# The lead of the row scores over the key scores in quad 0: fourteen units at first, two more per block

## The reference

```python
q, k, v = split_heads(x @ Wq.T + bq), ...          # 16 heads of 16 columns
q, k = rope(q), rope(k)
att = where(tril, einsum('bhqd,bhkd->bhqk', q, k) / 4, -inf)
y = einsum('bhqk,bhkd->bhqd', softmax(att), v)     # then @ Wo.T + bo
x = layernorm(x + y)
h = silu(x @ w1.T * s1) * (x @ w2.T * s2)          # 256 -> 1024
h = gelu(h @ h1.T * s)                             # 1024 -> 1024
h = gelu(h @ h2.T * s)                             # 1024 -> 1024
x = layernorm(x + h @ w3.T * s3)                   # 1024 -> 256
```

## Time and profile before

| | |
|---|---|
| median of three runs | 2791.91 us |
| the profiled execution's own time | 2795.36 us |
| its span | 2793.6 us |
| PE busy | 2729.1 us (98%) |
| VectorE (DVE) busy | 1899.9 us (68%) |
| ScalarE (ACT) busy | 1348.4 us (48%) |
| mean granted clock of PE | 0.989 |

### The profile page before, as it was taken

One profiled execution on the slowest core, in us unless ns is written; L12 is line 12 of the kernel. 1 busy time (PEld: TensorE's weight loads), 2 busy tenths in 40 slices (PEclk: granted clock), 3 DMA queues, 4 the chain that ended last, 5 costly groups with the idle time before them and its releaser, 6 DMA issues.

```text
span 2793.6 us, 39368 instructions
## 1 busy us (share of the span) xinstructions
PE 2729.1 (98%) x14880; PEld 1424.9 (51%) x14880; DVE 1899.9 (68%) x4003; ACT 1348.4 (48%) x2641; POOL 138.3 (5%) x206
## 2 busy tenths in 40 slices
PE   8899999999999999999999999999999999999998
PEld 4423333333333333333323333588888887888887
DVE  6999999888888888888887774633333352443343
ACT  4436666777776777777777776411111111000100
POOL 3300110001100001100000000000000000000000
PEclk9979999999999999999999999999999999999999
DMA  7731110001110011110001000411111132121100
GB/s 217 204 74 39 30 30 26 3 15 32 29 43 6 5 33 32 30 34 3 1 3 39 19 5 9 118 58 58 58 58 58 43 128 108 46 82 54 45 16 23
DMA packets 95613, 133.47 MB, mean 48 GB/s; under 512 B 31462, under 2 KB 69094, under 8 KB 91718
## 3 DMA queue, kind: packets, MB, share of 16 engines
q1 hardware_dynamic: 81452, 96.25, 10.7%
q0 software_dynamic: 6336, 23.34, 3.8%
q10 hardware_dynamic: 7648, 11.54, 1.5%
HBM read 83.77 MB, written 47.32 MB: 47 GB/s over the span
## 4 chain that ended last, share of the span: by engine, by line
PE 88%; DVE 6%; issue 2%; ACT 1%; DMA 1%; SPq 0%; ACTq 0%; POOLq 0%; POOL 0%; DVEq 0%
PE wi_f L984 19%; PE at_o L533 18%; PE at_row L498 17%; PE at_key L512 16%; PE na_h L1202 13%; PE na_y L1214 3%; DVE at_segmax L584 3%; DVE fr_masked L580 1%; DMA values<-pr_vals 1%; ACT at_probs L648 1%; PE at_key L515 1%; PE wi_p L833 1%; DVE pr_parts L252 0%; DVE pr_full L248 0%; PE pr_main L130 0%
## 5 line engine op out<-in xcount | busy, mean ns | idle before, releaser
L648 ACT ACTIVATE at_probs<-at_key 128x512 f32<-128x512 f32 (+3 forms) x2304 | 1127.3, 567 | 502.4 <-PE at_key L512 353.2
L584 DVE TENSOR_REDUCE at_segmax<-at_row 128x1 f32<-128x512 f32 x1792 | 1142.8, 684 | 169.2 <-PE at_row L498 164.9
L512 PE MATMUL at_key<-fr_q_stack,fr_k_stack 99*128 99x512 bf16 (+3 forms) x1152 | 415.0, 365 | 1.3 <-ACT at_probs L648 1.0
L498 PE MATMUL at_row<-fr_k_stack,fr_q_stack 96*128 96x512 bf16 (+3 forms) x1152 | 404.6, 376 | 10.8 <-DVE at_mask L612 5.5
L498 PE MATMUL at_row<-at_k_stack,at_q_stack 96*128 96x512 bf16 (+3 forms) x1152 | 408.1, 364 | 1.8 <-DVE at_segmax L584 1.1
L512 PE MATMUL at_key<-at_q_stack,at_k_stack 99*128 99x512 bf16 (+3 forms) x1152 | 402.2, 364 | 7.5 <-ACT at_probs L648 6.9
L1202 PE MATMUL na_h<-fr_h,fr_h2w_h 128*128 128x512 f32 x1024 | 322.1, 396 | 1.4 <-DVE fr_h L730 1.4
L533 PE MATMUL at_o<-at_probs,fr_values 128*32 128x512 f32 (+3 forms) x2304 | 289.0, 574 | 0.0
L533 PE MATMUL at_o<-at_probs,at_values 128*32 128x512 f32 (+3 forms) x2304 | 287.9, 572 | 0.0
L580 DVE CUSTOM_DVE_ANT_0 fr_masked<-at_row,fr_causal 128x384 f32<-128x384 f32 (+3 forms) x512 | 243.8, 483 | 45.1 <-PE at_row L498 44.7
L498 PEld LDWEIGHTS at_row<-fr_k_stack,fr_q_stack 96*128 96x128 bf16 x1152 | 110.3, 99 | 308.3 <-DVE at_segmax L584 160.1
(11 more groups left out here) (121 smaller groups left out, 2558.1 us busy)
## 6 DMA issues: line engine op xcount, KB each, us to landing
hidden<-wi_h SPq DMA_DIRECT2D x64, 256.0 KB, 2.0
na_h2f<-hidden SPq DMA_DIRECT2D x8, 1024.0 KB, 7.7
q_parts<-pr_parts SPq DMA_DIRECT2D x48, 128.0 KB, 2.4
k_parts<-pr_parts SPq DMA_DIRECT2D x48, 128.0 KB, 3.3
at_q_stack<-q_parts POOLq DMA_DIRECT2D x48, 128.0 KB, 3.5
at_k_stack<-k_parts POOLq DMA_DIRECT2D x48, 128.0 KB, 3.8
values<-pr_vals SPq DMA_DIRECT2D x32, 136.0 KB, 3.3
outputs<-at_outs SPq DMA_DIRECT2D x128, 34.0 KB
```

The source lines that it names most:

```text
L498: last = nc.tensor.matmul(bank[:, 0:w], qst[u][0:SROWS, c, h, i * P:(i + 1) * P], kst[u][0:SROWS, h, s * CH:s * CH + w], start=True, stop= ...
L512: last = nc.tensor.matmul(bank[:, q0:CH], kst[u][0:SROWS + PARTS, h, j * P:(j + 1) * P], qst[u][0:SROWS + PARTS, c, h, q0:CH], start=True, ...
L584: nc.vector.tensor_reduce(segmax[:, n % 2, h * TPC + i, s:s + 1], row_ps[r % RING_R][:, 0:w], op=ALU.max, axis=AX.X).then_inc(rows_taken, 1)
L648: nc.scalar.activation(probs[:, g % RING_P, h, q0:CH], key_ps[m % RING_K][:, q0:CH], ACT.Exp).then_inc(probs_ready, 1)
```

## The change

One constant is added, and the slack in the goal of `rows_before_keys` is the smaller of the old one and fourteen units plus two units for every block (n is the number of the key block). From block 7 on it is the old 28 units.

```diff
 SLACK = 28 * CH
+FIRST_SLACK = 14 * CH
 FIRST_EARLY = 3
...
-            goal = min(total, key_cols + lead + SLACK)
+            goal = min(total, key_cols + lead + min(SLACK, FIRST_SLACK + n * CH * 2))
```

## The result

The changed kernel takes 2804.63 us, the median of six runs (2803.88 to 2806.04); the kernel before took 2792.13 beside it (2791.44 to 2796.06). The ratio is 1.0044, 95% interval 1.0033 to 1.0055: 12.5 us slower. The forecast was 2799.0 with a range to 2803.5, so the direction was right and the size was not.

The account below looks back on a forecast made before the run. The prediction took VectorE to bound the beginning of the attention stage, with PE taking over gradually. Hole 7.3 less 1.0 saved gave +6.3, plus 0.7 for the clock: +7.0 us, forecast 2799.0, range 2790.5 to 2803.5.

Parts of the forecast that it names:

- Step 1: Before the first key score: fourteen rows fewer in front save nothing; it starts 0 to 0.5 us earlier, taken as 0.
- Step 2: Before the first key score: DVE idles from 151.15 to about 158.4 after row unit 36, 7.3 us.
- Step 3: Blocks 0 to 6: 6,912 missing columns repaid, 8.3 us at DVE's price, 3.0 at PE's; net with the hole +6.3 us.
- the saving of 1.0 us: DVE idle that extra rows take away: 0.64 us in blocks 5 and 6, another 0.4 us in block 1.
- Rival A: Quad 0: PE bounds the repayment, missing rows cost 3.0 us plus a 0.5 us restart; +3.5, 2795.4 us; chance 0.15.
- Step 4: Maxima of blocks 1 to 6: fewer units before their keys still cover store and reload; cost 0.
- Step 5: Near 166, block 0's keys: closing operations of block 1 delay the rise of PE's clock; +0.7 us, ends 0 and +3.4.
- Rival C: Quad 0: clock low through most of block 0, or one more fall near a closing operation; +10.4, 2802.3 us; chance 0.16.
- Rival B: Quad 0: not slower, as the clock's falls at 186 and 230 vanish; -0.2, 2791.7 us; chance 0.12.

Follow-up runs that it names:

- the late shift: Changed kernel with 32 matmuls of 128 columns, results unused, on PE in front of the first key unit of quad 1: 2804.32 us, ratio 1.0036.
- the store first: Changed kernel with SyncE's loads of chunk 3 moved from in front of the first maxima to behind their reload: 2797.64 us, ratio 1.0020.
- The pair with filler: Sixteen unused matmuls ahead of each transpose of maxima, in the changed kernel (2817.74 us, ratio 1.0095) and in the kernel before (2815.78 us, 1.0084).
- the filler in the hole: Changed kernel with 56 matmuls of 128 columns, results unused, on PE in front of the first key unit: 2804.20 us, ratio 1.0046.
- the split load of the values: Changed kernel with chunk 3's loads behind the first maxima and quad 0's values loaded in two parts, the second behind the maxima: 2795.37 us, ratio 1.0009.

## Why the prediction was right in kind and short in size

**What bounds quad 0: shown.** VectorE's work, plus its idle time. Filling its idle with moved row units made quad 0 shorter, and holes made it longer.

**Step 1, start of the keys: right.** The first key score gained nothing: 24.06 us after the first row matmul, against 23.67 and 24.41 in the two executions of before. The cause is also shown: it waits for maxima that stand behind the loads of chunk 3. Without those loads in front it came at 18.65. The fixed cost of 2.0 us that the prediction quotes from the Trainium skill, "DMA: Bandwidth & Descriptors", section on the anatomy of one DMA, stands there for DMAs that GpSimd issues, and this reload is SyncE's. In the changed kernel the first key score starts 1.8 us after the reload is issued, so the 1.3 us of the trace was the better term.

**Step 2, the hole: right.** 7.3 us forecast, 7.79 measured. What a hole costs is also shown: 3.5, 4.3 and 8.3 us for holes of 3.3, 4.2 and 7.5.

**Step 3, the repayment: at VectorE's price, and the saving of 1.0 us did not come.** At the start of block 1 the changed plan is 6,272 columns short. In the execution with the late shift blocks 1 to 6 took 7.4 us longer than in the second execution of before, and so they did with the store first: 1.2 ns per column, VectorE's price. (Both have a fall between 194 and 202 that the kernel before lacks, with 1.4 to 1.5 us of idle of VectorE, and lack its fall at 230, worth 1.4; the two nearly cancel.) Quad 0 as a whole grew by 472.78 - 462.16 = 10.6 us, and DVE's waits by 36.1 - 26.3 = 9.8 us. The bookkeeping by idle time holds to 0.8 us here and to 1.4 us between the two executions of before (28.6 and 26.3 us of waits for 3.7 us of time). The pair with filler gives 5.9 at a hole of 6.13, a saving of 0.2 us where I had 1.0. Rival A (the repayment at PE's price, +3.5) is out.

**Step 4, later maxima: right.** PE waited for maxima once, at block 0.

**Step 5, PE's clock: this step failed.** I valued it at +0.7, with 3.4 as the upper end, and I counted one place. The runs show falls at three places of quad 0 and one of quad 1. In quad 0 those at 170 and 286 cost some 2.4 us together; the one at 198 is not priced by itself, and VectorE's idle in its stretch, 1.54 us, is about its upper end. The kernel before also loses 1.4 at 230, which the changed one does not: some 2.5 net. In quad 1, which I left out because the order of the work does not change there, the difference between the kernels grows by 3.0 us at the output store behind the fall (2.8 from mark 2 to mark 3). Together that is over 5 us where the sum had 0.7. Rival C, one more fall near a closing operation, had +10.4 for quad 0 and came nearest there (10.6); it too had nothing for quad 1. Rival B's sign is there as well: the clock stays at 0.98 or more from 186 to 198 and at 1.00 at 230, so both falls of the first profile are gone. But the one behind the closing operations of block 2 is back at 198, where these operations now stand, and those at 170 and 286 are new; B's gain did not come. The Trainium skill, "TensorE: Matmul & The Clock Gate", part 1, says that activity releases the clock and that the throttled state is the default. The rows from 162 to 170 show the clock rise once keys and values run; the fall at 170 came although PE had been busy 2.10 of the 4 us before it. I had used the section only for the stretch in front of the key.

**The base.** The profile that I read had a fall worth 3.7 us in quad 0 that the second profile does not have. Counted against that one execution, quad 0 grew by 6.9 us, which looks like the forecast of +7.0, but only because a fall in either kernel stands in the count; counted against the second one it grew by 10.6. The forecast was added to the median as if the median execution had the falls of the profiled one. That it has not is argued, not shown: of the 94 executions of the kernel before that were timed beside the experiments, 22 took over 2795 us, as the profiled one did (2795.36), and none of the 94 has a trace.

**The sum as measured**, profile against the second profile of before: start of the stage -1.3, quad 0 +10.6, to mark 3 +2.8, 12.1 us in the spans (2803.5 - 2791.4). The -1.3 has nothing to do with the change, since the first mark varies by more than that behind the same work. Of quad 0, 7.8 are the hole and some 2.5 the falls, net; the remaining 0.3 is not resolved.

**What stays open.** Why a given kernel's clock falls near 880 or 190 and another's, with the same order of work there, does not. The changed kernel had the fall near 880 in both profiles, the move of SyncE's loads kept it, the filler in the hole and the split load of the values lost it, and a shift of 1.8 us gave it to the kernel before, as did the filler at the transposes (0.87 and 0.79 from 870) and the 128 columns more per masked unit (0.83 from 860). That speaks for the moment at which PE pauses, not for the lead. No run sets that moment alone, so it is not shown. Also open is what the short lead costs in block 0 beside the hole once the hole is small.

## What to carry to other kernels

Before shortening a lead, look up when the thing that the lead waits for arrives: if a transfer fixes the start, less work in front of it only opens a hole, and where the engine that idles in it is the one that bounds the stage, the hole costs its full length. When the forecast adds to a median, ask first which events of the profiled execution the median does not have; where the profiled execution lies over the median by as much as a term of the sum, a second profile is worth more than a finer sum. Idle time of the bounding engine in one part of a block is worth filling with work from another part: here the median fell by 4.4 us, and quad 0 of the trace by 3.0 to 4.4.

## What was not expected of the hardware

PE's clock fell after waits of at most 1.4 us, where it had been high: busy 2.10 of 4 us at 166, 0.57 in the next stretch. The same kind of wait did not always bring a fall: in the second execution of the kernel before, PE was busy 2.56 of 4 us at 186, and the next stretch shows 1.00. A fall of this kind cost 1.4 (at 230) to 3.7 us (at 186 to 198) even where VectorE bounds, because at the low level PE becomes the later one: VectorE was busy 1.99 of 4 us at 194 in the first profile, 3.98 in the second. And a store of 12 KB took 8.1 to 8.8 us to land behind some 0.8 MB of chunk loads and the values' 1.1 MB, where the median one takes 1.3 us.
